# A GNN kernel's second layer: its first three aggregations moved beside the last tile of the first layer

## The reference

```python
def gcn_conv(x, W, b, src, dst, n):
    h = x @ W
    deg = jax.ops.segment_sum(jnp.ones(src.shape[0], h.dtype), dst, num_segments=n) + 1.0
    dinv = deg ** (-0.5)
    coef = dinv[src] * dinv[dst]
    agg = jax.ops.segment_sum(h[src] * coef[:, None], dst, num_segments=n)
    agg = agg + h * (dinv * dinv)[:, None]
    return agg + b
...
x1 = layer_norm(jax.nn.relu(gcn_conv(x, W1, b1, src, dst, n)), g1, beta1)
x2 = layer_norm(jax.nn.relu(gcn_conv(x1, W2, b2, src, dst, n)), g2, beta2)
x3 = layer_norm(jax.nn.relu(gcn_conv(x2, W3, b3, src, dst, n)), g3, beta3)
...
x = x + _L0_gnn_ref(xn, edge_index, ...) + _L0_mix_ref(xn[None], ...)[0]
x = x + _L0_ffn_ref(_layernorm(x, axis=-1)[None], ...)[0]
```

## Time and profile before

| | us |
|---|---|
| median of 3 runs | 1815.27 (1814.68 to 1818.9) |
| the profiled execution's own time | 1807.26 |
| its span in the trace | 1805.4 |
| layer 1's last aggregation starts, in the trace | 1199.44 |
| layer 2's aggregations begin | 1213.68 |
| layer 2 aggregates tile after tile until | 1529.03 |

### The profile page before, as it was taken

The page is one execution under the profiler, slowest core; times in us unless marked ns, Lnnn a source line. Parts: engine busy times, 40 slices in busy tenths (PEclk is TensorE's granted clock), DMA queues, the critical chain, the costliest instruction groups (busy, mean ns, idle before and its releaser), DMA issues.

```text
span 1805.4 us, 19204 instructions
## 1 busy us (share of the span) xinstructions
PE 1234.7 (68%) x6591; PEld 795.7 (44%) x6591; DVE 732.1 (41%) x1558; ACT 477.4 (26%) x1003; POOL 538.8 (30%) x579
## 2 busy tenths in 40 slices
PE   4973010110001018888999999999999999999796
PEld 4641000000000005555656666666666666566375
DVE  7860020000000007878555545554333233688634
ACT  5340000000011006486332222221211111344164
POOL 3177777766667770000100000021023000000143
PEclk9985555555555558999999999999999999999898
DMA  9820000000000000003132222213333333564311
GB/s 281 283 74 0 0 1 0 0 0 0 0 0 0 1 0 1 1 1 83 48 104 61 73 67 61 58 52 99 87 89 88 78 92 87 141 165 123 91 42 29
DMA packets 82936, 111.25 MB, mean 62 GB/s; under 512 B 51871, under 2 KB 67348, under 8 KB 82872
## 3 DMA queue, kind: packets, MB, share of 16 engines
q1 hardware_dynamic: 62344, 106.98, 21.5%
q0 software_dynamic: 20528, 3.47, 1.4%
HBM read 76.08 MB, written 27.67 MB: 57 GB/s over the span
## 4 chain that ended last, share of the span: by engine, by line
PE 59%; issue 29%; DVE 5%; ACT 4%; another core or an unknown queue 2%; DMA 0%; POOL 0%; DVEq 0%; ACTq 0%; SPq 0%; POOLq 0%
PE psum L2088 58%; PE psum L2468 1%; ACT big L1751 0%; ACT scr L1768 0%; ACT acc L1643 0%; ACT scr L1758 0%; PE psum L2461 0%; ACT scr L1925 0%; ACT scr L1794 0%; DVE big L930 0%; DVE scr L930 0%; DVE scr L1499 0%; DMA scr<-in_src_pad 0%; ACT scr L1775 0%
## 5 line engine op out<-in xcount | busy, mean ns | idle before, releaser
L728 POOL DMA_INDIRECT counts<-big,eidx x416 | 416.2, 1000 | 194.1 <-issue 158.6
L2088 PE MATMUL psum<-rows,scr 125*125 125x512 f16 x1250 | 274.5, 379 | 3.6 <-DVE rows L1299 1.6
L2088 PE MATMUL psum<-big,scr 125*125 125x512 f16 x1250 | 274.6, 379 | 1.0 <-DVE big L1322 1.0
L909 DVE TENSOR_TENSOR acc<-acc,scr 128x2000 bf16<-128x2000 bf16 x26 | 31.2, 1199 | 457.5 <-remote 455.2
L2088 PEld LDWEIGHTS psum<-rows,scr 125*125 125x125 f16 x1250 | 170.2, 136 | 103.3 <-issue 2.9
L2088 PEld LDWEIGHTS psum<-big,scr 125*125 125x125 f16 x1250 | 169.7, 136 | 96.7 <-DVE big L1322 1.5
L2088 PE MATMUL psum<-acc 128*32 128x125 bf16 (+2 forms) x516 | 52.8, 263 | 206.0 <-issue 202.0
L2088 PE MATMUL psum<-wb,scr 128*125 128x512 f16 x600 | 137.0, 379 | 2.0 <-DVE scr L1305 1.4
L2088 PEld LDWEIGHTS psum<-acc 128*32 128x32 bf16 (+1 forms) x516 | 31.9, 121 | 226.6 <-issue 220.0
L2088 PE MATMUL psum<-scr,wm 128*128 128x313 f32 x48 | 22.9, 573 | 140.0 <-ACT scr L1768 110.6
L753 POOL TENSOR_TENSOR acc<-acc,wm 125x256 f32<-125x256 f32 x25 | 17.1, 731 | 319.6 <-DVE acc L1311 319.6
(11 more groups left out here) (415 smaller groups left out, 1872.6 us busy)
## 6 DMA issues: line engine op xcount, KB each, us to landing
scr<-counts SPq DMA_DIRECT2D x75, 683.6 KB
counts<-wb SPq DMA_DIRECT2D x25, 683.6 KB
counts<-big,eidx POOLq DMA_INDIRECT x416
scr<-counts SPq DMA_DIRECT2D x75, 79.3 KB
scr<-in_x SPq DMA_DIRECT2D x25, 125.0 KB
picked<-big SPq DMA_DIRECT2D x5, 566.6 KB
rows<-in_x SPq DMA_DIRECT2D x5, 560.0 KB
out<-acc SPq DMA_DIRECT2D x5, 560.0 KB
```

The lines of the kernel that those rows point to most:

```text
L728: pool.indirect_dma_start(cells, bass.IndirectOffsetOnAxis(ap=eidx[:, r * EQ + g:r * EQ + g + 1], axis=0), evalue[:, at_c:at_c + 1], None, ...
L909: done.did(dve.tensor_tensor(ohp, free(edp16, b * DB, [[2, DB // 2], [0, P], [1, 2]]), free(iop, 0, [[0, DB // 2], [2, P], [1, 2]]), ALU.i ...
L2088: return pe.matmul(o, l, r, start=start, stop=stop)
```

## The change

Layer 1's last four tiles leave the loop on every engine. On TensorE the row blocks of layer 2's tiles 0, 1 and 2 are laid among the pieces of layer 1's last steps. A third PSUM bank (2) holds tile 2, and tiles 0 and 1 change places between banks 0 and 1 (`bank2_of`). SP fetches the slabs of tiles 0 and 1 ahead of layer 1's last one. VectorE takes the tail in another order: in particular add_mix(24) comes after turned_y_low(24), and L1388 of tiles 0 and 1 is done ahead of both normalisations. product3(0) and product3(1) both move into tile 3, ahead of rows 8 and 18; from tile 4 on product3(t-2) stands ahead of row 5 again.

```diff
@@ -413,6 +413,10 @@
     def bank(b, p, n, o=0):
         return psum[:p, b, o:o + n]
 
+    def bank2_of(t):
+
+        return 2 if t == 2 else (t + 1) % 2
+
     def z_parts(c, h):
 
         b = 2 + c % 2 * 3
@@ -592,7 +596,7 @@
         for layer in range(3):
             base = layer * T
 
-            for t in range(HEAD):
+            for t in range(2 if layer == 1 else 0, HEAD):
                 if base + t >= RING:
                     sp.wait_ge(sem("agg_done"), base + t - RING + 1)
                 if layer == 0:
@@ -631,15 +635,23 @@
                     if layer == 2 and t in (10, 15, 20):
                         store_staged((t - 10) // G)
                 continue
-            with sp.Fori(0, LOOPS) as i:
+            with sp.Fori(0, LOOPS - 1) as i:
                 for k in range(HEAD, HEAD + RING):
-                    sp.wait_ge(sem("agg_done"), i * RING + (base + k - RING + 1))
-                    if layer == 0:
-                        landed(i * RING + k)
-                    fetch(i * RING + k, (base + k) % RING)
-                    if layer == 0:
-                        sp.wait_ge(sem("fx_done"), i * RING + (k - RING + 1))
-                        fetch_x(i * RING + k, k % RING)
+                    sp.wait_ge(sem("agg_done"), i * RING + (k - RING + 1))
+                    landed(i * RING + k)
+                    fetch(i * RING + k, k % RING)
+                    sp.wait_ge(sem("fx_done"), i * RING + (k - RING + 1))
+                    fetch_x(i * RING + k, k % RING)
+            for t in range(T - RING, T):
+                sp.wait_ge(sem("agg_done"), t - RING + 1)
+                if t == T - 1:
+                    for k in range(2):
+                        sp.wait_ge(sem("agg_done"), T + k - RING + 1)
+                        fetch(k, (T + k) % RING)
+                landed(t)
+                fetch(t, t % RING)
+                sp.wait_ge(sem("fx_done"), t - RING + 1)
+                fetch_x(t, t % RING)
 
         store_staged(NC - 2)
         store_staged(NC - 1)
@@ -1363,16 +1375,25 @@
                 add_mix(1, 1, 16)
             if t >= 2:
                 add_mix(t, t % RING, 16 + t // RING * 16)
-        with dve.Fori(0, LOOPS) as i:
+        with dve.Fori(0, LOOPS - 1) as i:
             done.enter(i, 4 * 4)
             for k in range(HEAD, HEAD + RING):
                 step1(i * RING + k, k % 2, k % RING, i * 16 + (16 + k // RING * 16))
-            done.leave(LOOPS)
-        for t in (T - 2, T - 1):
-            if t == T - 1:
-                turned_x_low(t)
-            rows2_sum(t)
-            rows2_low(t)
+            done.leave(LOOPS - 1)
+        for t in range(T - RING, T - 1):
+            step1(t, t % 2, t % RING, 16 + t // RING * 16)
+        turned_x_low(T - 2)
+        rows2_sum(T - 3)
+        rows2_low(T - 3)
+        sum_rows(T - 1, (T - 1) % 2)
+        turned_y_low(T - 1)
+        add_mix(T - 1, (T - 1) % RING, 16 + (T - 1) // RING * 16)
+        rows2_sum(T - 2)
+        hidden1(T - 1)
+        rows2_low(T - 2)
+        turned_x_low(T - 1)
+        rows2_sum(T - 1)
+        rows2_low(T - 1)
 
         def normalise(t, buf, width, relu, xhat):
             dve.wait_ge(sem(relu), t + 1)
@@ -1380,18 +1401,25 @@
             dve.tensor_scalar(buf, buf, mv2[:, 0:1], rs2, ALU.subtract, ALU.mult).then_inc(sem(xhat), 1)
 
 
-        def step2(t, b, before=2, last=False):
-            if before >= 2:
-                rows3_out(t - 2)
+        def rows2_out(t, b, home):
+            dve.wait_ge(sem("agg_done"), t + (T + 1))
+            dve.scalar_tensor_tensor(out=pre[b][:, 0:D2], in0=bank(home, P, D2), scalar=d2out[:, bass.ds(t, 1)],
+                                     in1=b2r, op0=ALU.mult, op1=ALU.add).then_inc(sem("pre2_done"), 1)
+
+        def step2(t, b, home, last=False):
+            rows3_out(t - 2)
             if not last:
-                dve.wait_ge(sem("agg_done"), t + (T + 1))
-                dve.scalar_tensor_tensor(out=pre[b][:, 0:D2], in0=bank(b, P, D2), scalar=d2out[:, bass.ds(t, 1)],
-                                         in1=b2r, op0=ALU.mult, op1=ALU.add).then_inc(sem("pre2_done"), 1)
+                rows2_out(t, b, home)
                 normalise(t, pre[b][:, 0:D2], D2, "relu2_done", "xhat2_done")
                 rows3_in_low(t, b)
 
-        for t in range(HEAD + RING):
-            step2(t, t % 2, min(t, 2))
+        for t in range(2):
+            rows2_out(t, t, bank2_of(t))
+        for t in range(2):
+            normalise(t, pre[t][:, 0:D2], D2, "relu2_done", "xhat2_done")
+            rows3_in_low(t, t)
+        for t in range(2, HEAD + RING):
+            step2(t, t % 2, bank2_of(t))
         dve.wait_ge(milestone("fnorm_done"), AFTER["fnorm_done"])
         done.did(dve.tensor_scalar(f_back, fnorm[:, 0:2], 1e-20, 1.0 / F16_TOP, ALU.max, ALU.mult))
         done.did(dve.tensor_scalar(g_back, fnorm[:, 0:1], float(D) ** 0.5, fnorm[:, 2:3], ALU.mult, ALU.add))
...
@@ -1955,11 +1983,18 @@
             hidden1(t)
             if t == 2:
                 mixed_scales()
-        with act.Fori(0, LOOPS) as i:
+        with act.Fori(0, LOOPS - 1) as i:
             for k in range(HEAD, HEAD + RING):
                 step1(i * RING + k, k % 2)
+        for t in range(T - RING, T - 1):
+            step1(t, t % 2)
+        turned_x(T - 2)
+        rows2_high(T - 3)
+        halve_rows(T - 1, (T - 1) % 2)
+        turned_y(T - 1)
+        rows2_high(T - 2)
+        hidden1(T - 1)
         turned_x(T - 1)
-        rows2_high(T - 2)
         rows2_high(T - 1)
 
         def ffn_norms():
@@ -2536,28 +2571,56 @@
         product2(2)
         product1(4)
         turn_x(3)
-        with pe.Fori(0, LOOPS) as i:
+        with pe.Fori(0, LOOPS - 1) as i:
             for k in range(HEAD, HEAD + RING):
                 step1(i * RING + k, k, i)
-
-        def step2(t, k, i, first=False):
-            b = k % 2
-            previous = [
-
-                (12, lambda: product2(T - 2)), (16, lambda: turn_x(T - 1)), (21, lambda: product2(T - 1)),
-                (T - 3, lambda: pe.wait_ge(sem("lo2_done"), T - 2)),
-                (T - 2, lambda: pe.wait_ge(sem("lo2_done"), T - 1)),
-                (T - 1, lambda: pe.wait_ge(sem("lo2_done"), T))] if first else [
-                (5, lambda: product3(t - 2, 16 * (k - 1) if i is None else i * (16 * RING) + 16 * (k - 1)))]
-            if not first and isinstance(t, int) and t == 1:
-                previous = ()
-            aggregate(1, t, k, b, wide, loads(1, k, i), "pre2_done", free_from(t, k, i), previous)
-
-        pe.wait_ge(sem("lo2_done"), T - 3)
+        for t in range(T - RING, T - 1):
+            step1(t, t, None)
+
+        def wide_rows(t, lo, hi):
+
+            for s in range(lo, hi):
+                pe.wait_ge(sem("lo2_done"), s + 1)
+                for h in range(len(wide)):
+                    last = mm(bank(bank2_of(t), P, 512), ring[(T + t) % RING][:, s, :], wide[h](s),
+                              s == 0 and h == 0, s == T - 1 and h == len(wide) - 1)
+            if hi == T:
+                last.then_inc(sem("agg_done"), 1)
+
+        pe.wait_ge(sem("ring_loaded" + str(T % RING)), loads(1, 0, None))
+        pe.wait_ge(sem("y_done"), T - 1)
+        wide_rows(0, 0, 16)
+        product2(T - 3)
+        turn_x(T - 2)
+        wide_rows(0, 16, T - 3)
+        aggregate1(T - 1, T - 1, None)
+        product2(T - 2)
+        turn_y(T - 1)
+        wide_rows(0, T - 3, T - 2)
+        product1(T - 1)
+        pe.wait_ge(sem("ring_loaded" + str((T + 1) % RING)), loads(1, 1, None))
         pe.wait_ge(sem("y_done"), T)
-        for t in range(HEAD):
-            step2(t, t, None, first=t == 0)
-        for t in range(HEAD, HEAD + RING):
+        wide_rows(1, 0, T - 2)
+        turn_x(T - 1)
+        pe.wait_ge(sem("ring_loaded" + str((T + 2) % RING)), loads(1, 2, None))
+        pe.wait_ge(sem("yT_done"), T)
+        wide_rows(2, 0, 16)
+        wide_rows(0, T - 2, T - 1)
+        wide_rows(1, T - 2, T - 1)
+        product2(T - 1)
+        wide_rows(2, 16, T - 1)
+        for t in range(3):
+            wide_rows(t, T - 1, T)
+
+        def step2(t, k, i):
+
+            def turned_product3(n):
+                return lambda: product3(t - n, 16 * (k - n + 1) if i is None else i * (16 * RING) + 16 * (k - n + 1))
+
+            between = [(8, turned_product3(3)), (18, turned_product3(2))] if k == 3 else [(5, turned_product3(2))]
+            aggregate(1, t, k, bank2_of(k), wide, loads(1, k, i), "pre2_done", free_from(t, k, i), between)
+
+        for t in range(3, HEAD + RING):
             step2(t, t, None)
         pe.wait_ge(sem("fsquares_done"), 1)
         for n, columns in enumerate(((0, 1), (2, 3), (4,))):
```

## The result

The changed kernel takes 1826.96 us (median of 7 runs, 1820.08 to 1834.66) against 1815.27 us (7 runs, 1810.78 to 1820.66): a ratio over all runs of 1.0059, 95% interval 1.004 to 1.0078 (the ratio of the two medians is 1.0064). It is slower, by 11.7 us between the medians, where +12.2 was forecast. That the two numbers agree is in good part luck: the stretch that the change touches grew by 6.75 us in the profile, the largest term of the forecast didn't come, and what fills the place of that term in the medians stands in no row of the changed code.

What follows compares the result with a forecast made beforehand. It took TensorE's issue to bound the kernel, so idle time there moves the end. Terms of 15.0 us less 2.8 gave +12.2 us on the median 1815.27, so 1827.5 us; range over all cases 1819 to 1832.

Steps and rivals of the forecast that it cites:

- The two gaps of before: TensorE's idle gaps of 1.60 and 1.19 us at the layer 1 to 2 handover would go: -2.8 us.
- Step a: At the handover, product1(24) comes before VectorE has finished its input yT: TensorE waits 0.6 us.
- Step b: Tile 24's normalisation is held until GpSimd's 25 additions end, so TensorE waits for turn_x(24): 5.8 us, bounds 0 to 6.3.
- the first rival: Tile 24's normalisation slips in among GpSimd's additions at no cost; chance 0.14, half on either side of 1820.7 us.
- Step c: At the start of tile 3, TensorE waits for bank 0 until tile 1's pre2_done: 0.8 us.
- Step d: In tile 3, product3(0) comes before its DMA-transposed rows land: 3.3 us, bounds 3.1 to 4.6.
- Steps e and f: In tile 3, product3(1) waits for its transpose, 2.5 us (0 to 5); the clock falls, 2.0 us (0 to 4).

Runs made afterwards that it cites:

- e10: e8 with the loads of f1 and f2 issued ahead of layer 2's first transpose: 1812.58 us against 1816.79 for the kernel before, ratio 0.9984.
- e1: The kernel before, unchanged, measured against itself on another chip: 1289.75 us against 1289.06, ratio 1.0006.
- e9: The kernel before with one settled memset ahead of GpSimd's 25 additions: 1815.03 us (one run).
- e11: The changed kernel with add_mix(24) put back ahead of turned_y_low(24) on VectorE: 1825.59 us against 1816.79 for the kernel before, ratio 1.0049.
- e3: The changed kernel with the first products with W3 (product3 of tiles 0 to 3) placed later: 1288.65 us, ratio 0.9999 to the kernel before.
- e4: The changed kernel with 14 idle matmuls ahead of tile 3's first product with W3: 1295.98 us, ratio 1.0057 to the kernel before.
- e2: The changed kernel, unchanged, run again on another chip: 1295.11 us, ratio 1.0047 to the kernel before.
- e7: The changed kernel with the loads of f1 and f2 moved behind the third transpose: 1292.68 us, ratio 1.0019 to the kernel before.
- e12: The kernel before with 30 settled memsets ahead of GpSimd's 25 additions: 1821.27 us (one run).
- e8: The changed kernel with e7's and e3's edits, more rows ahead of product1(24), tiles 0 and 1 completed earlier: 1290.01 us, ratio 1.0005 to the kernel before.

## Why the prediction was right in sum and wrong in parts

**The two gaps of before.** Right: -2.8 us; both are gone, and e10 shows the work without gaps at the 326.7 us that follow from it.

**Step a** (0.6). Right: 0.64.

**Step b, the step that failed** (5.8 us). It said of the normalisation of tile 24 that "it was held until the stream's last instruction" and would be so again. The first half is right, also on a second chip and with the stream shifted (e1, e9). The second is wrong: a request 6.8 us into the stream was served in 1.27 us, and the step cost 0. I made a rule out of a single row. What the row lacked is a second request at another distance, and the forecast moved the request from 11.8 to 6.8 us into the stream without asking whether that matters. Had it been shut out, the price would have been as worked out, 1234.51 + 17.14 + 0.55 - 1246.57 = 5.6 us; e11 shows the length (5.61) but not the price, since there the stream was earlier. The lower bound, "0 (if it slips in)", the case of the first rival (chance 0.14), was what happened. The ten normalisations that were served ended 0.55 to 0.61 us after the end of the addition in progress. The four that were shut out ended 0.55 us after the stream's last, through seven additions more. So neither length is the rule for such a stream, and no run shows what makes the difference.

**Step c** (0.8). Right: 0.89.

**Step d** (3.3). Right: 3.15. Tile 0 was complete at Y = 1264.3, TensorE arrived at Y + 5.2 and went on at Y + 8.4, as forecast. e3 takes the gap away by giving the transpose its time.

**Steps e and f** (2.5 + 2.0). Here terms were mis-sized, and they aren't two terms. I took the middle of 0 to 5 for e; the runs show the upper bound, with `product3(1)` at Y + 18.9 ("near Y + 19"). That is 4.8 us behind the Y + 14.1 at which TensorE would have come at full clock, and e4 shows just this gap, 4.74 us in the bracket and 4.9 by starts. In the changed kernel the fallen clock takes 3.0 of these 4.8 us and the gap 1.85; with the clock kept up (e4) the whole is a gap. So the clock's loss ahead of the landing cost nothing by itself here; what fell behind it added: in e2 3.4 us at 0.50, in e11 5.8, half of which is lost. With f1 and f2 out of the way (e7) the second gap is 0, the lower bound; so that gap came with these two loads. The 2.0 us of f are an estimate that no run shows. The gap of b didn't come, and the clock fell once in the changed kernel, to 0.50 within d's gap of 2.98 us, a place that stood only in the upper bound of f; it stayed there for 6.8 us, which cost 3.0. The row quoted against a fall after a shorter gap, 2.56 us of idle time, ran from 778.8 to 781.4 and so not wholly within 777 to 781; this changes nothing here.

**The sum.** Forecast 15.0 less 2.8; the handover shows 9.5 less 2.8, or +6.75 us (8.8 in e2, and 9.9 in e11, which differs by one line). That b was 5.8 too high and e with f 0.35 too low makes a forecast of 5.5 us too much, and the same sum with b at 0 and no fall of the clock, 12.2 - 5.8 - 2.0 = +4.4, would have been 2.4 too low because of e and the clock. So the forecast met the median's +11.7 us by luck: its mechanism would have put 12.2 us into the handover, where at most 9.9 were seen. That the median came to +11.7 us and not 7 to 10 isn't shown by any row of the changed code. Part of it may be that the profile of the changed kernel is that of its fastest run, 1820.08 us, and that the same TensorE program took 2.1 us more of handover in e2, where the clock fell at other moments. The interval, 7.3 to 14.2 us, overlaps with that of e11 (5.6 to 12.0), holds the 8.8 and the 9.9, and barely misses the 6.75; the end of the common part stands at 1199.4, 1205.8 and 1211.8 in three profiles of the program before (bare, e9, e12) and at 1206.6, 1208.8 and 1208.9 in three of the changed one and its variants (bare, e11, e10). How much of the difference is such scatter stays open.

## What to carry to other kernels

Starting a stage earlier only pays if the chains behind its first tiles get their time as well: here 2.8 us of idle time were removed, and a DMA transpose asked for 3.1 us too early and a second one behind 2 MB of weights in the same queue cost 8.0 us with the clock that fell. Give such a first consumer the place that its chain's rows add up to, and look where bulk loads stand among the small urgent transfers: f1 and f2 issued 7.5 to 7.9 us ahead of the first transpose left no gap (e10, transposes landing after 3.1 to 3.9 us), behind the first one they made the second land after 7.6 (the changed kernel), behind the third one the fourth after 6.8 (e8). And a stall that a trace shows once is a fact about its place; before pricing it elsewhere, look for a second instance at the distance to which it is moved, or shift it by an experiment.

## What was not expected of the hardware

- A VectorE normalisation of 125 x 1024 fp32, which takes 0.81 us in tile 23's step, took 5.61 to 6.08 us and ended 0.55 us after a stream of 25 GpSimd additions of 0.72 to 0.75 us when it started 11.6 to 12.1 us into the stream (before, e1, e9, e11), and took 0.81 to 1.29 us, ending 0.55 to 0.61 us after the end of the addition in progress, when it started 6.5 to 7.1 us into it (the other ten profiles). In these ten the VectorE operation behind it took 1.21 or 1.22 us, against 0.74 with the stream over (before), and the two additions in which these rows ended took 1.17 to 1.23 instead of 0.72.
- The clock didn't follow the length of a gap alone. It fell to 0.50 within the gap of 2.98 us of the changed kernel, about 1.3 us after the end of one of 2.96 us (e2), and not at all at one of 2.97 us (e11). The windows of e11 across that gap and the next one, of 4.46 us, in which it did fall:

```profile
1274.00:1275.00 1.00, 0.00 (x0) 0.00 (x0) 0.00 (x0) 0.00 (x0) 0.00 (x0) 1.00 1.15 168
1276.00:1277.00 1.00, 1.00 (x10) 0.91 (x9) 0.81 (x2) 0.00 (x0) 0.00 (x0) 1.00 1.05 401
...
1284.00:1285.00 1.00, 0.00 (x0) 0.00 (x0) 0.00 (x0) 0.00 (x0) 0.00 (x0) 0.77 0.95 243
1290.00:1291.00 1.00, 1.00 (x4) 0.58 (x3) 0.00 (x0) 0.00 (x0) 0.00 (x0) 0.50 1.02 195
```

- A transpose that landed 3.1 us after its issue in the median of 25, and also behind one fetch (e7), took 7.58 us behind f1, f2 and a fetch, 8.9 in e4 and 9.3 in e2.
- The same program takes 1289 us on two chips, and 1815 in the first measurement and on the chip of e9 to e12. The difference lies in the stretch in which GpSimd scatters the counts. That stretch is as long in both (96 to 673 us in the kernel before, 97 to 675 in e1), but from 140 to 700 us TensorE was busy for 82 us in the one, at a granted clock of 0.51, and for 520 us in the other, at 0.98. Why stays open.
